# TensorE's and ScalarE's work on finished blocks, moved within the first edge pass of a graph network

## What is computed

```
h = relu(layernorm(x))
q, k, v = projections of h                       # 8 heads of 16
scores  = sum(q[dst] * (k[src] + rel_bias[edge_type])) / SCALE
exp_s   = exp(scores - seg_max[dst])
out     = segment_sum(exp_s / (seg_sum[dst] + 1e-8) * v[src], dst)
x       = x + out @ Wo + bo                      # then layernorm, relu and
                                                 # the second layer's projection
```

## Time and profile before

| | |
|---|---|
| median of 3 runs | 7942.78 us (7936.55 to 7952.53) |
| the profiled execution, whole | 7937.73 us |
| its span in the profile | 7936.0 us |
| first edge pass, from block 0 to the last scatter | about 1160 to 2850 us of the span |
| mean granted TensorE clock | 0.69 |

### The profile page before, as it was taken

The page is one execution under the profiler, slowest core; times in us unless marked ns, Lnnn a source line. Parts: engine busy times, 40 slices in busy tenths (PEclk is TensorE's granted clock), DMA queues, the critical chain, the costliest instruction groups (busy, mean ns, idle before and its releaser), DMA issues. The chain is left out here.

```text
span 7936.0 us, 112987 instructions
## 1 busy us (share of the span) xinstructions
PE 2893.9 (36%) x28649; PEld 2358.6 (30%) x28650; DVE 4600.8 (58%) x10704; ACT 1481.2 (19%) x3863; POOL 3660.9 (46%) x4402
## 2 busy tenths in 40 slices
PE   4179633455655532344233431345200000001334
PEld 3168512344545422334223431334200000000122
DVE  9677435566666636677467865677444444443333
ACT  0123100111111121222212222344311111110000
POOL 0155223333332324565445544554466666654555
PEclk9999996666777766676666766667555555555677
DMA  0034223334343523345333443334332222222334
GB/s 21 10 90 107 63 80 95 95 103 104 94 97 86 99 63 70 76 88 76 72 75 80 82 77 68 75 75 79 48 51 51 52 52 53 51 49 61 73 84 81
DMA packets 293996, 576.70 MB, mean 73 GB/s; under 512 B 137262, under 2 KB 182043, under 8 KB 273827
## 3 DMA queue, kind: packets, MB, share of 16 engines
q0 software_dynamic: 113232, 255.82, 21.2%
q1 hardware_dynamic: 142642, 278.18, 11.4%
q10 hardware_dynamic: 38049, 41.86, 1.7%
HBM read 479.10 MB, written 29.32 MB: 64 GB/s over the span
## 5 line engine op out<-in xcount | busy, mean ns | idle before, releaser
L3053 PE MATMUL bank<-tab,oh 128*128 128x136 bf16 x11700 | 894.3, 249 | 654.6 <-PEq L3045 387.2
L3053 PEld LDWEIGHTS bank<-tab,oh 128*128 128x128 bf16 x11700 | 865.0, 111 | 714.6 <-issue 714.5
L1422 PE MATMUL bank<-ident,hid 128*128 128x128 f32 x125 | 55.8, 447 | 2636.6 <-issue 1297.8
L1422 PEld LDWEIGHTS bank<-ident,hid 128*128 128x128 f32 x125 | 22.7, 182 | 2683.4 <-issue 2683.4
L2791 POOL DMA_INDIRECT land_a<-table,idx_a x624 | 665.3, 1066 | 228.4 <-issue 166.4
L2810 POOL DMA_INDIRECT land_r<-table,idx_r x492 | 502.5, 1021 | 214.9 <-issue 149.4
L2901 DVE TENSOR_TENSOR prod<-prod 128x128 f32<-128x128 f32 (+4 forms) x621 | 536.5, 864 | 14.6
L2976 ACT ACTIVATE rows<-bank 128x408 f32<-128x408 f32 x936 | 397.8, 515 | 753.9 <-ACTq L2975 554.9
L2602 PE MATMUL bank<-tab_l,oh_l 128*128 128x128 bf16 x3846 | 404.7, 240 | 210.3 <-issue 103.5
L2887 DVE TENSOR_TENSOR prod<-rows,bank 128x5376 f32<-128x5376 f32 x75 | 431.6, 5755 | 51.5 <-DVEq L2886 39.5
L3312 PE MATMUL bank<-tab_l,oh_l 128*128 128x384 bf16 x1250 | 260.1, 378 | 445.6 <-PEq L3306 333.2
(11 more groups left out here) (512 smaller groups left out, 8558.2 us busy)
## 6 DMA issues: line engine op xcount, KB each, us to landing
loc<-el_loc SPq DMA_DIRECT2D x78, 1088.0 KB
loc_l<-el_loc SPq DMA_DIRECT2D x52, 1088.0 KB
typ_l<-el_typ SPq DMA_DIRECT2D x52, 672.0 KB
rows_r<-land_r SPq DMA_DIRECT2D x123, 272.0 KB
landings_l<-landings_l SPq DMA_DIRECT2D x41, 784.0 KB
attr<-in_edge_attr ACTq DMA_DIRECT2D x75, 343.8 KB
land_a<-table,idx_a POOLq DMA_INDIRECT x936
land_r<-table,idx_r POOLq DMA_INDIRECT x492
```

What stands on the lines that cost most here:

```text
L3053: last = pe.matmul(got[g % full][:, (c - of[0]) * W1:(c - of[0] + 1) * W1], oh[:, o], tab[:, t, x], start=n == 0, stop=n == len(parts) - 1 ...
```

## The change

TensorE's loop over runs now holds, for the next run, all of its keys and values: `early_keys`, second half, `values`. The first run's second half and values stand before the loop. So the finished blocks' work comes behind the next run's values and ahead of the run after it. On ScalarE `exps(0)` of the next run is put behind the turns of this one, so that `to_conv`, `node_update` and `keep_sums` lie between the exponentials of a run and the `take_landed` that follows it. At the end TensorE works through the keys and values of the padding run, and VectorE hands every bank back.

```diff
@@ vector @@
                     finish()
+                    dve.sem_inc(s("shifted"), 1)
+                    dve.wait_ge(s("exped"), 1)
+                    dve.sem_inc(s("exped"), -1)
+                    for n in range(len(key_groups) + len(value_groups)):
+                        dve.wait_ge(s(f"bank_full{n % len(banks)}"), 1)
+                        dve.sem_inc(s(f"bank_full{n % len(banks)}"), -1)
+                        if n < len(key_groups) + len(value_groups) - len(banks):
+                            dve.sem_inc(s(f"bank_free{n % len(banks)}"), 1)
...
-                    for n in range(AHEAD):
-                        dve.wait_ge(s(f"bank_full{n}"), 1)
-                        dve.sem_inc(s(f"bank_full{n}"), -1)
@@ scalar @@
                         with act.Fori(r0, r1) as r:
-                            exps(0)
                             turns = turns_of_overflow(act, r)
                             take_landed(r + 1)
                             with act.Fori(0, turns):
                                 exps(MC - MORE)
+                            exps(0)
...
+                    exps(0)
                     runs_of_block(0)
@@ tensor @@
                         with pe.Fori(r0, r1):
+                            early_keys()
                             keys(groups_of_keys[AHEAD:])
                             values()
-                            early_keys()
...
                     early_keys([0])
+                    keys(groups_of_keys[AHEAD:])
+                    values()
                     block_of(0)
```

## The result

| | before | changed |
|---|---|---|
| median | 7939.66 us (4 runs, 7934.08 to 7952.53) | 8042.57 us (4 runs, 8030.08 to 8056.4) |
| ratio, 95% interval | | 1.0135 [1.0112, 1.0159] |
| profiled execution, whole | 7937.73 us | 8040.85 us |
| blocks 2 to 9, each | 73.6 | 73.2 |
| blocks 10 to 23, each | 57.3 | 64.2 |

The changed kernel is 1.35% slower; 8042.57 lies 12 us above the predicted range. The last scatter of the pass comes 116.7 us later: -6.1 by the start of block 2, -3.4 in blocks 2 to 9, +95.6 in blocks 10 to 23, +30.6 after the start of block 24. Some 14 us of that are won back in the later passes, which no experiment here touches.

What follows compares the result with a forecast made beforehand. TensorE, short of instructions while GpSimd gathers, was taken as the bound. Blocks 10 to 23 +1, blocks 2 to 9 -16, end of pass +24 gave +9 us on the median 7943: 7952 us, 8-in-10 range 7895 to 8030.

Steps and rivals of the forecast that it cites:

- What bounds the kernel: First edge pass: while GpSimd gathers, instructions reach TensorE slowly, and VectorE waits 12.4 us a block for keys.
- First part: One-turn block, end of keys to start of GpSimd's gather window: 29.4 us, 9.1 more than before.
- Window: One-turn block, start of GpSimd's gather window to its last gather: 21.5 us, bounds 20.5 and 22.4.
- Third part: One-turn block, last gather to end of the next keys: 7.3 us, 8.1 less than 15.4; bounds 4.1 and 9.
- the forecast's +1: Blocks 10 to 23, all 14 together: +1 us, kept between -43 and +42.
- Bounds of the ring: One-turn block, end of keys to end of next keys: 58.2 against 58.1 us, +0.1, bounds -3.1 and +3.
- Blocks 2 to 9: Eight blocks with keys ending sooner, 2.0 us each: -16 us; bounds -5.5 and +1 each.
- End of the pass: Padding run's keys and values delay the first of the last three `to_conv`: +24 us, bounds 18 and 28.
- rival 3: Slower, ScalarE becomes the bound: First part 31, Third part 8.9, +81 us, 8024 us; chance 0.20.
- Rival 4: Move does nothing for the second half of keys: Third part stays 15.4, +139 us, 8082 us; chance 0.07.
- rival 1: TensorE has its instructions before the window, VectorE sets the pace: blocks 44.6 for 57.3, 7773 us; chance 0.08.

Runs made afterwards that it cites:

- k4: Kernel before with seven of eight first gathers and six of eight per overflow turn left out, GpSimd memsets in their place; 7533.47 us, single run.
- k18: Kernel before with SyncE's one-hot loads held until GpSimd has issued the eight first gathers; 8026.95 us, ratio 1.0039.
- k17: Changed kernel with SyncE's one-hot loads held until TensorE's landed groups begin, so they are in flight when the window begins; 8103.74 us, ratio 1.0143.
- k1: Changed kernel, but TensorE waits for its landed rows itself instead of for ScalarE's `keys_in`; 7887.86 us, ratio 0.9942.
- k13: Kernel before with the next run's early keys put in a loop of one turn, so a branch stands ahead of them; 7919.77 us, single run.
- k6: k1 without the padding run's keys, values and exponentials; 7925.35 us, ratio 0.9905.
- k5: Kernel before with TensorE's share of `land_a_free` incremented behind the second half of keys, so the gathers begin after these; 7927.25 us, ratio 0.9905.
- k7: k6 with the landed rows' buffer given free behind the second half of keys, as in k5; 7937.32 us, ratio 0.9920.
- k8: Changed kernel with as many gathers, each 33 or 32 floats wide instead of a whole row; 8079.36 us, single run.
- k9: Changed kernel with eight GpSimd memsets (5.0 us) between its waits and its first index copy in each run; 8113.79 us, ratio 1.0146.
- k10: k6 with the 5.0 us of GpSimd memsets of k9 ahead of each run's first index copy; 8003.04 us, ratio 1.0008.
- k12: Same kernel as k5, profiled beside the kernel before on one chip; 7926.02 us, single run.
- k11: The kernel before itself, unchanged, profiled beside k12 on one chip; 7992.0 us, single run.
- k15: Changed kernel with TensorE's code shifted by 64 idle semaphore instructions ahead of the pass; 8030.17 us, single run.

## Why the prediction was wrong, point by point

- **What bounds the kernel** was right: TensorE's instructions come slowly in the window, and VectorE waits. k4 puts a number on it: 13 us of a one-turn block in the order before. That it is instructions TensorE lacks is inferred, as said above.
- **First part**: 29.4 predicted, 31.7 measured. In block 18's ring the chain of finished blocks' work took 14.35 us (2437.91 to 2452.26) for 13.2, and ScalarE's jump and loads of bounds 2.33 for the 1.1 that I took from TensorE's jump. Right mechanism, 2.3 us too small: 14 times, 32 us.
- **Window**: 21.5 predicted, 20.6 measured, -13 us in all. The reason that I gave, no one-hot loads beside the index copy, was wrong: k18 has none and its copy takes 1.04 us and its window 22.3, k17 has them and 0.19 and 20.6. It goes with VectorE's work beside it, which no run isolates.
- **Third part**: 7.3 predicted, bound 9, measured 12.6. This is the failed step: 14 times 5.3 is 74 us of the 95 that blocks 10 to 23 took beyond the forecast's +1. Its three terms: 139 to 153 matmuls were to be through at the last gather, 109 were (mean of 14, at 20.6 us). The resumption was to take 1 us, and at full pace took 3.2. The rest was to run at 14 per us, and ran at 9.5 for 6 us (57 matmuls) before it reached 18. The first term was carried over from a one-turn window of the order before (109 in 6.8 us), where it is typical of the 14, into an order in which the windows give fewer, 74 in 6 us. No row of before shows that difference, and its cause is open. But the earlier trace rows, 75 in 15 us in block 1, which the text quoted, came nearer: as a bound it would have left 143 matmuls, 10 us at 14 per us, and a third part of 12.
- **Bounds of the ring**: -3.1 to +3 was too narrow; it was +7.4 by the mean rings, and +6.8 a block by the block starts. The bounds of the third part took in two rates of the window, but not the clock after it (the 14 per us are from a stretch at 0.77) nor the time to resume.
- **Blocks 2 to 9**: -2.0 each predicted, -0.4 measured. Keys ended earlier (block 2: 21.3 for 23.0 after its start), and most was given back behind them: the landed copy waits for ScalarE's chain (27.7 after the keys' end for 18.4 in block 2, 29.2 for 18.9 in block 9), and the turns follow.
- **End of the pass**: +24 predicted. From the end of block 24's keys to the first of the last three `to_conv` it was 2934.37 - 2881.00 = 53.4, for 27.6 before: +25.8. The other 5 us of the +30.6 are block 24's own late keys, a fifteenth ring that the sum didn't count.
- **Rivals**: rival 3 gave 8024, the nearest, with the first part at 31 and the third at 8.9. Its mechanism, ScalarE late for the landed copy and for the turn's exponential, is there: that exponential comes 0.33 us after the copy at 2456.03, and VectorE waits 2.1 us a block for it (28.9 in 14). But k1 shows that its weight lay on TensorE's keys, held back by `keys_in`, and not on the turns. Rival 4, the third part unchanged, is refuted by k1 and by the 12.6; rival 1 by the window's 46 matmuls in 18.8 us.
- **What would have told it beforehand**: the text named `keys_in` as the wait that moves TensorE's landed groups from 14.6 to 24.5, and costed that as a longer first part. It didn't ask what else those 10 us were used for. In k1 TensorE gets 108 matmuls through in the same time, before the window.

The Trainium skill's rule on instruction supply (Runtime: NRT & Kernel Launch, section Instruction fetch mechanics: filled ahead in blocks, mostly hidden) doesn't hold in a window of gathers, if the "issue" gaps are missing instructions: the changed kernel's TensorE gets 46 matmuls in 18.8 us there. The Trainium skill's remark in the same section on taken branches found no support in k13, as far as its branch is one that is taken.

## What to carry to other kernels

Before moving work past a step, list what each engine waits for with that step's release, and cost the wait on the engine that has the most instructions still to issue: here one semaphore turned a change worth -0.6% (k1) into +1.35%. Where TensorE must issue hundreds of instructions beside GpSimd's indirect gathers, what counts is how many of them are left when the gathers begin; what is left went at 2 to 3 per us here and ran at the lower clock afterwards, and free PSUM banks bound how far it can run ahead. The cheapest repairs are letting TensorE wait for its own data (k1, 0.9942), with that not computing the padding run (k6, 0.9905), and, in the order before, holding the gathers back until the keys are out (k5, 0.9905); the hold on top of k6 adds nothing (k7, 0.9920).

## What the runs showed of the hardware

- While GpSimd issues indirect gathers, TensorE of the changed kernel gets 66 to 71 matmuls, each with its load, and then 46 in 18.8 us (k8: 42 in 16.8; k9: 33 in 18.8). How many come before the gaps is a number and not a time: k10 got its 62 in 8.5 us at a clock of 0.63, block 18 of k1 its 70 in 13.0. In the order before there are 102 to 121, and in k12 44 came in 5.1 us in the middle of a window.
- Gathers 33 floats wide (k8, 12 GB/s) do this as much as those of whole rows (87 GB/s). One-hot loads in flight don't bring it on sooner: in the order before 109 matmuls went through in 6.8 us at a DMA share of 1.00 and 217 GB/s, and k17 got its 66 at 0.96 and 258 GB/s.
- In the changed kernel's block 18 TensorE ran without gaps again 3.2 us after the start of the last gather, and the granted clock was 0.50 for 6 us after that, then 1.00.
- A GpSimd copy of 8 columns takes 0.19 us in the changed kernel, and 0.89 to 1.13 in k18, where VectorE is busy 4.49 of 5.00 us; the eighth gather is issued 9.8 and 11.5 us after the window's start.
- The kernel before itself lay between 7922 and 8001 us beside different groups of kernels, with 59.6 us for a one-turn block in k11 where the first profile has 57.3; the changed kernel's one-turn blocks and those of its near variants (k8, k15 to k17) were 64.1 to 64.9.
